# Layer 0's attention: q's product and the turned values change places in a ring of three PSUM banks, and the ring's empty place moves ahead of v's second chunk

## The chip, the cores and the metric

The kernel runs on one core of a Trainium2 chip as one program. The metric is the device time of one execution in microseconds (us). Three runs of the kernel before took 2770.33, 2770.84 and 2774.33 us; the median is 2770.84 us.

## The reference, cut to what matters

The model has four layers, each a cross attention and a feed-forward net on x of 16 batches x 112 rows x 256. Only the attention of layer 0 is touched. For each batch b it computes, with 8 heads of 32:

```
xn = layernorm(x)                       # 112 x 256
q  = xn @ wq.T + bq ; k = ctx @ wk.T + bk ; v = ctx @ wv.T + bv   # ctx: 375 x 256
p  = softmax(q k^T / sqrt(256)) ; o = p v                         # per head
res = o + q ; ln = layernorm(res) * g + b
out = silu(ln) @ base_w.T + b_splines(ln) @ (spline_w * scaler).T # 8 spline bases per value
x  = x + tanh(gate) * out
```

The values and the sums are the same before and after the change.

## The kernel before, in words

The program goes through eight stages one after the other (attention and net of each of four layers). In the attention of layer 0 (`attention_stage` with `kan=True`) each engine runs an instruction list of its own, written out batch by batch by `batches`; they meet only at semaphores. TensorE (PE) does all products and transposes, ScalarE (ACT) and VectorE (DVE) copy the results out of PSUM and do the softmax, the norms and the splines' arithmetic, GpSimd (POOL) does powers, squares and sums.

The stage is a software pipeline. In round t the program works on several batches at once: it turns (transposes) the probabilities of batch t and multiplies them with the values, prepares batch t+1 (`xT`, `k`, `q`, `v`, `qtok`), finishes the attention output of batch t-1 (`oback`, `lnt`) and does the splines of batch t-2 (`kan`). `LAG` says which batch a use belongs to. Rounds run from -1 to 17; in rounds 2 to 14 all uses are there.

A round has two halves, one for each group of four heads, and each half has the positions 0 to 3. The head of a half is `scores` (L807) and `pv` (L838). At positions 1 to 3 stands one `turn` each (four transposes of probabilities, L820), followed by the uses that the table `CYCLES` lists there:

- `xT`: the normed rows turned (L727). `k` (L712, four matrix products) and `v` (L720, four) of one chunk. `q` (L735, eight). `qtok`: q turned back to rows (L742, two).
- `oback`: the attention output turned back to rows (L758, two). `lnt`: the normed residual turned (L763, two). `kan`: the product with silu (L773, four), and right behind `lnt` the 32 spline products (L780).

All these results go through three PSUM banks, `full_ps`, in a strict ring: the n-th place of the list gets bank n mod 3. `rest` is a place that holds nothing and only moves the count on. `bank_free` makes PE wait before each use until the previous content of that bank is copied out. Who copies:

- ACT, in a fixed order in the first half: `xT` (L903), the first turn (L938), `o` out of its own bank (L946), the exponentials of heads 0 and 1 (L931), `k` (L892), the exponential of head 2, `q` (L921), that of head 3, `v` (L898), `k`. At a round's end, behind the splines' arithmetic, the two `v` of position 3.
- DVE, in the first half: two maxima of scores (L1152), one cube (L1245), the second turn's copy (L1172), `oback` (L1198), the third turn's copy (L1172), the sum with `qtok` and the statistics, a second cube, silu (L1240). In the second half: two maxima, the normed residual (L1214) that `lnt` needs, the turn's copy, and at the round's end the update of x (L1188, it reads `kan`), the last turn's copy (L1172), the next normed rows (L1075), `qtok` (L1103), statistics (L1193) and the rows of the net's norm (L195).

The lists of ACT and DVE put `oback` and `q`, and `qtok` and `v`, on different engines, so they don't depend on the order of these in `CYCLES`.

Of the kernel before, what the change touches and what calls it, by code (L numbers as in the profile page):

```python
# [222 lines left out]
def batches(eng, body, tail):  # L223

    for b in range(-1, B + tail):
# [3 lines left out]


CYCLES = {
    0: [[[("xT",)], [("k", 0)], [("q", 0), ("oback",)], [("v", 0, 0), ("k", 1)]],
        [[], [], [("kan",), ("lnt",)], [("v", 1, 0), ("qtok",), ("v", 2, 0), ("rest",)]]],
# [2356 lines left out]
```

How the kernel before makes its waits and increments, by code:

```python
    def settle(self, dve, b, count):  # L173
        core = self.core
        dve.bn_aggr(core.mv[:, b, :], core.row_stats[:, b, :]).then_inc(self.s_mv.sem, 1)
        dve.wait_ge(self.s_mv.sem, count + 1)
        if self.layer == 2:
            dve.tensor_scalar(core.rstd[:, b], core.mv[:, b, 1:2], 1.0 + RMS_EPS, EPS * RMS_EPS, ALU.mult, ALU.add)\
                .then_inc(self.s_var.sem, 1)
        else:
            dve.tensor_scalar(core.rstd[:, b], core.mv[:, b, 1:2], EPS, None, ALU.add).then_inc(self.s_var.sem, 1)
# [1 line left out]
    def root(self, pool, b, count):  # L185
        pool.wait_ge(self.s_var.sem, count + 1)
        pool.tensor_tensor(self.core.rstd[:, b], self.core.rstd[:, b], self.core.minus_half[:], ALU.pow)\
            .then_inc(self.s_root.sem, 1)
# [1 line left out]
    def apply(self, eng, b, count):  # L191
        core = self.core
        eng.wait_ge(self.s_root.sem, count + 1)
        eng.tensor_scalar(core.normed[:, b, :], core.x_all[:, b, :], core.mv[:, b, 0:1], core.rstd[:, b, :],
                          ALU.subtract, ALU.mult).then_inc(self.s_rows.sem, 1)
# [11 lines left out]
    def rows_in(self, eng, b):  # L208
        if b >= EARLY:
            eng.wait_ge(self.s_rows.sem, b - EARLY + 1)
# [330 lines left out]
                def load(b, par, known):  # L542
                    if known:
                        sp.wait_ge(s_job.sem, s_job.at(b - 2, index_of[kv[-1]]))
                        sp.sem_inc(s_tick[2].sem, 1)
                        sp.dma_start(ctxT[:, par], dram["ctxT"][b]).then_inc(s_ctx[par].sem, 16)
```

## Time and profile before

| | |
|---|---|
| median of three runs | 2770.84 us |
| the profiled execution | 2773.1 us, its span 2771.3 us |
| attention of layer 0 | about 10 to 410 us of the span |
| one round in its steady part | 21.7 us |
| PE busy over the whole span | 95% |

The profile is of one execution. Times in rows count from the start of the span. "[0.19 <-ACT a_qT L921]" behind a row is the idle time of the engine right before it and what ended it. PE's ends are modelled, so on PE the distance from one start to the next tells more than the durations. "PEld" is PE's weight load, and L numbers are lines of the kernel.

### The profile page before, as it was taken

Reading aid. Unit: us, or ns where it says so; the run is one execution under the profiler, and the core shown is the slowest. Engines: PE = TensorE matmul, PEld = TensorE weight load, DVE = VectorE, ACT = ScalarE, POOL = GpSimd, SP = SyncE. Lnnn points to the kernel's source line nnn. Section 1 sums busy time; section 2 is a strip of 40 time slices with the busy share of each in tenths; the row PEclk is TensorE's granted clock in tenths of the full one; section 3 lists DMA queues with packets and bytes.
Section 4 is the critical chain, followed back from the end, with each engine's and each line's share of the span. In section 5 each row is a group of like instructions: output and inputs, shape, how many; then the busy total and the mean of one; then the engine's idle time right before and its main releaser. Section 6 shows DMA issues by size and latency. Waiting matters only on the chain. (4 is left out here: it accounts for less than half of the span.)

```text
span 2771.3 us, 56714 instructions
## 1 busy us (share of the span) xinstructions
PE 2625.3 (95%) x19818; PEld 1983.4 (72%) x19818; DVE 1544.7 (56%) x4177; ACT 1301.0 (47%) x3610; POOL 643.8 (23%) x626
## 2 busy tenths in 40 slices
PE   6999978999999999989899998999998999979998
PEld 4777755666666666656666666999996777768887
DVE  4778746555555555536777774333325777842222
ACT  4777733343334434421566663333335777732222
POOL 1666661000000000000444431222221111113332
PEclk9999989999999999989999998999999999999999
DMA  4000002000000000010000006999992000059896
GB/s 124 18 18 18 12 16 94 13 13 7 13 7 13 7 13 7 1 34 1 21 18 20 22 7 219 330 325 332 326 328 58 24 18 24 7 197 311 304 313 224
DMA packets 91811, 267.57 MB, mean 97 GB/s; under 512 B 25068, under 2 KB 50804, under 8 KB 77268
## 3 DMA queue, kind: packets, MB, share of 16 engines
q1 hardware_dynamic: 74356, 242.53, 25.3%
q0 software_dynamic: 13632, 18.62, 3.1%
q10 hardware_dynamic: 3616, 3.67, 0.4%
q8 instruction: 128, 2.10, 0.3%
q14 instruction: 79, 0.65, 0.1%
HBM read 248.13 MB, written 16.65 MB: 96 GB/s over the span
## 5 line engine op out<-in xcount | busy, mean ns | idle before, releaser
L820 PEld LDWEIGHTS a_full_ps<-ident,a_probs 112*125 112x125 f32 x2688 | 367.0, 189 | 129.7 <-issue 64.5
L1917 PEld LDWEIGHTS m_banks<-m_x_inT,m_w 128*128 128x128 f32 x3824 | 435.1, 192 | 15.2 <-issue 13.5
L1917 PE MATMUL m_banks<-m_x_inT,m_w 128*128 128x128 f32 x3824 | 442.2, 276 | 1.4 <-ACT m_x_inT L1988 0.9
L931 ACT ACTIVATE a_probs<-a_masked,a_negmax 112x375 f32<-112x375 f32 x512 | 305.4, 598 | 287.7 <-DVE a_negmax L1146 287.7
L820 PE MATMUL a_full_ps<-ident,a_probs 112*125 112x112 f32 x2688 | 417.3, 281 | 18.3 <-ACT a_pT L938 5.6
L1172 DVE COPY a_pT<-a_full_ps 125x448 f32<-125x448 f32 x448 | 277.5, 621 | 222.1 <-PE a_full_ps L820 217.2
L720 PE MATMUL a_full_ps<-attention_room 128*125 128x256 f32 (+1 forms) x960 | 331.1, 474 | 9.8 <-ACT a_qT L921 3.9
L712 PE MATMUL a_full_ps<-attention_room 128*128 128x375 f32 x896 | 324.0, 490 | 13.8 <-PEq L1760 8.6
L1146 DVE CUSTOM_DVE_ANT_0 a_masked<-a_sc_ps,a_mask_add 112x375 f32<-112x375 f32 x512 | 249.8, 545 | 33.2 <-PE a_sc_ps L807 32.0
L931 ACT ACTIVATE a_probs<-a_sc_ps,a_negmax 112x375 f32<-112x375 f32 x384 | 217.0, 577 | 91.1 <-DVE a_negmax L1152 91.1
L838 PEld LDWEIGHTS a_o_ps<-a_pT,a_v 125*32 125x32 f32 (+1 forms) x5376 | 164.5, 118 | 126.5 <-issue 98.1
L807 PE MATMUL a_sc_ps<-a_kT,a_qT 32*112 32x375 f32 (+1 forms) x1792 | 241.7, 514 | 7.2 <-ACT a_probs L931 3.8
L1928 PE MATMUL m_banks<-m_w,m_hid 128*128 128x256 f32 x992 | 232.9, 383 | 0.0
L720 PEld LDWEIGHTS a_full_ps<-attention_room 128*125 128x125 f32 x960 | 165.9, 189 | 89.8 <-issue 65.6
L838 PE MATMUL a_o_ps<-a_pT,a_v 125*32 125x112 f32 (+1 forms) x5376 | 216.3, 265 | 6.3 <-DVE a_pT L1172 2.6
L712 PEld LDWEIGHTS a_full_ps<-attention_room 128*128 128x128 f32 x896 | 159.8, 194 | 84.9 <-issue 15.5
L1152 DVE TENSOR_REDUCE a_negmax<-a_sc_ps 112x2 f32<-112x750 f32 x192 | 171.2, 933 | 79.1 <-PE a_sc_ps L807 79.1
L2002 ACT ACTIVATE m_silu<-m_banks,m_b 128x128 f32<-128x128 f32 x280 | 102.7, 368 | 239.4 <-PE m_banks L1917 231.7
L1928 PEld LDWEIGHTS m_banks<-m_w,m_hid 128*128 128x128 f32 x992 | 179.9, 190 | 32.0 <-issue 11.9
L2146 DVE SCALAR_TENSOR_TENSOR m_hid<-m_banks,m_b,m_silu 128x128 f32<-128x128 f32 x280 | 98.0, 351 | 157.8 <-ACT m_silu L2002 157.8
L2002 ACT ACTIVATE m_silu<-m_banks 128x128 f32<-128x128 f32 x216 | 59.6, 276 | 213.0 <-PE m_banks L1917 213.0
L938 ACT ACTIVATE a_pT<-a_full_ps 125x448 f32<-125x448 f32 x224 | 120.0, 536 | 62.6 <-PE a_full_ps L820 61.1
(253 smaller groups left out, 3451.8 us busy)
## 6 DMA issues: line engine op xcount, KB each, us to landing
m_w<-in_L2f_w SPq DMA_DIRECT2D x105, 1024.0 KB, 6.8
m_w<-in_L3f_w SPq DMA_DIRECT2D x72, 768.0 KB, 4.8
attention_room<-in_ctxT SPq DMA_DIRECT2D x64, 375.0 KB, 3.1
m_w<-in_L3f_w SPq DMA_DIRECT2D x36, 640.0 KB, 5.6
m_b<-in_L2f_b SPq DMA_DIRECT2D x35, 128.0 KB, 7.9
p_rows<-normed SPq DMA_DIRECT2D x16, 224.0 KB, 6.3
attention_room<-in_L0x_spline_wT SPq DMA_DIRECT2D x1, 2048.0 KB, 10.3
net_room<-in_L1f_w SPq DMA_DIRECT2D x2, 1024.0 KB
```

Of the source, the lines that this page charges most:

```text
L712: mm = pe.matmul(use_ps[:, 0:SK], wk[:, c, u[1] * P:(u[1] + 1) * P], ctxT[:, par, c, :], start=(c == 0), stop=(c == DC - 1))
L720: mm = pe.matmul(use_ps[0:KT, 0:v_width], ctxT[:, par, c, k * KT:(k + 1) * KT], wv[:, c, part * v_width:(part + 1) * v_width], start=(c == ...
L807: pe.matmul(sc_ps[:, a, 0:SK], lhs, kT[r:r + k, par, c, :], start=True, stop=True)\
L820: mm = pe.transpose(full_ps[0:KT, bank_of["turn", i, k], (j % 4) * S:(j % 4 + 1) * S], probs[:, i % 2, a, t * KT:(t + 1) * KT], ident[0:S, ...
L838: mm = pe.matmul(o_ps[a % WIDE * VW:(a % WIDE + 1) * VW, block * S:(block + 1) * S], v[:, par, t, head(i, a), :], pT[:, i % 2, KC * a + t, :],
L931: act.activation(probs[:, i % 2, a, 0:SK], src, ACT.Exp, bias=negmax[:, m:m + 1], scale=-1.0 if mask else 1.0, accum_out=rowsum[:, par, n: ...
L1146: dve.tensor_tensor_reduce(out=masked[:, i % 2, a, :], in0=sc_ps[:, a, 0:SK], in1=bias, scale=-1.0, scalar=FLT_MAX, op0=ALU.add, op1=ALU.m ...
L1152: dve.tensor_reduce(negmax[:, m:m + 2], sc_ps[:, 2 * a:2 * a + 2, 0:SK], AX.X, ALU.max, negate=True).then_inc(s_max.sem, 1)
L1172: dve.tensor_copy(pT[:, i % 2, 4 * k:4 * (k + 1), :], full_ps[0:KT, bank_of["turn", i, k], 0:4 * S] .rearrange("p (j s) -> p j s", j=4)).t ...
L1917: mm = pe.matmul(ab_ps[:, (par * FC + f) % RING, i * SLOTS:(i + 1) * SLOTS], w[:, par, c, f * P:(f + 1) * P], x_inT[:, c, :], start=(c == ...
L1928: mm = pe.matmul(y_ps[:, par, 0:D], hid[parts[f], f, :], w2[parts[f], par, f, :], start=(f == 0), stop=(f == FC - 1))
L2002: act.activation(silu[parts[f], i, :], ab_ps[0:r, i, 0:SLOTS], ACT.Silu, bias=b1[0:r, par, f:f + 1] if biased else 0.0).then_inc(s_silu.se ...
```

## The change

Two lists of layer 0's table change; no other line does.

```
CYCLES = {
-    0: [[[("xT",)], [("k", 0)], [("q", 0), ("oback",)], [("v", 0, 0), ("k", 1)]],
-        [[], [], [("kan",), ("lnt",)], [("v", 1, 0), ("qtok",), ("v", 2, 0), ("rest",)]]],
+    0: [[[("xT",)], [("k", 0)], [("oback",), ("q", 0)], [("v", 0, 0), ("k", 1)]],
+        [[], [], [("kan",), ("lnt",)], [("rest",), ("v", 1, 0), ("v", 2, 0), ("qtok",)]]],
```

`v 0` is v's first chunk, `v 1` its second. The order of PE's work follows the list: `oback` is now ahead of `q`, and `qtok` behind `v 2`. The banks follow as well (T is a turn):

```
before  xT0 T1 k0:2 T0 q:1 oback:2 T0 v0:1 k1:2 | T0 T1 kan:2 lnt:0 T1 v1:2 qtok:0 v2:1 rest:2
after   xT0 T1 k0:2 T0 oback:1 q:2 T0 v0:1 k1:2 | T0 T1 kan:2 lnt:0 T1 rest:2 v1:0 v2:1 qtok:2
```

So these waits on a bank change: `oback` waited for k0's copy and now for the first turn's; `q` waited for the first turn's copy and now for k0's; `v0` waited for q's copy and now for oback's; `k1` for oback's and now for q's; `v1` for kan's (the update of x) and now for lnt's; `qtok` for lnt's and now for kan's; the next round's `xT` for qtok's and now for v1's, and its `k0` for v1's and now for qtok's. No instruction is added or taken away.

## Rows read from the trace of the kernel before

**Rows 1.** Page, part 1: busy time of each engine over the span.
```profile
PE 2625.3 (95%) x19818; PEld 1983.4 (72%) x19818; DVE 1544.7 (56%) x4177; ACT 1301.0 (47%) x3610; POOL 643.8 (23%) x626
```

**Rows 2.** Windows: stretch, length, busy PE, PEld, DVE, ACT, POOL, granted clock, DMA share, GB/s.
```profile
200.00:340.00 140.00, 137.51 (x1057) 101.82 (x1060) 111.45 (x208) 103.23 (x233) 90.78 (x59) 1.00 0.06 18
39.00:42.00 3.00, 3.00 (x7) 2.06 (x7) 0.00 (x0) 0.64 (x3) 0.00 (x0) 0.50 0.03 5
```

**Rows 3.** Waits of PE, 0 to 400 us: total us, times, longest.
```profile
PE a_full_ps L720 <- ACT a_qT L921: 3.9, 16, 0.7
...
PE a_full_ps L720 <- DVE x_all L1188: 1.8, 12, 0.2
```

**Rows 4.** Timeline of PE, first half of a steady round: start, us, what.
```profile
247.21 0.59 PE L820 MATMUL a_full_ps<-ident,a_probs 112*125 112x112 f32 x4
247.63 1.06 PE L735 MATMUL a_full_ps<-a_xT,attention_room 128*128 128x112 f32 x8
...
248.55 0.43 PE L758 MATMUL a_full_ps<-ident,a_oT 128*112 128x128 f32 x2
248.82 0.59 PE L820 MATMUL a_full_ps<-ident,a_probs 112*125 112x112 f32 x4
...
249.60 1.13 PE L720 MATMUL a_full_ps<-attention_room 128*125 128x256 f32 x4 [0.19 <-ACT a_qT L921]
```

**Rows 5.** Timeline of ACT in the same half.
```profile
247.91 0.59 ACT L892 ACTIVATE a_kT<-a_full_ps,attention_room 128x375 f32<-128x375 f32 x1
...
248.91 0.63 ACT L921 ACTIVATE a_qT<-a_full_ps,attention_room 128x112 f32<-128x112 f32 x2
```

**Rows 6.** Timeline of DVE in the same round, up to the normed residual.
```profile
247.83 0.62 DVE L1172 COPY a_pT<-a_full_ps 125x448 f32<-125x448 f32 x1
...
249.45 0.62 DVE L1172 COPY a_pT<-a_full_ps 125x448 f32<-125x448 f32 x1
...
254.80 0.41 DVE L1214 TENSOR_SCALAR a_resn<-a_res,a_mv,a_rstd 112x256 f32<-112x256 f32 x1
```

**Rows 7.** Timeline: the residual turned in a late round, then in the steady one.
```profile
211.41 0.42 DVE L1214 TENSOR_SCALAR a_resn<-a_res,a_mv,a_rstd 112x256 f32<-112x256 f32 x1
...
211.97 0.38 PE L763 MATMUL a_full_ps<-ident,a_resn 112*128 112x112 f32 x2 [0.26 <-DVE a_resn L1214]
...
255.35 0.38 PE L763 MATMUL a_full_ps<-ident,a_resn 112*128 112x112 f32 x2
```

**Rows 8.** Timeline of PE at that round's end.
```profile
262.51 0.59 PE L820 MATMUL a_full_ps<-ident,a_probs 112*125 112x112 f32 x4
...
263.25 1.13 PE L720 MATMUL a_full_ps<-attention_room 128*125 128x256 f32 x4 [0.15 <-DVE x_all L1188]
...
264.22 0.38 PE L742 MATMUL a_full_ps<-ident,a_qT 128*112 128x128 f32 x2
264.44 1.03 PE L720 MATMUL a_full_ps<-attention_room 128*125 128x256 f32 x4
```

**Rows 9.** Timeline of DVE and POOL at that round's end.
```profile
263.14 0.62 DVE L1172 COPY a_pT<-a_full_ps 125x448 f32<-125x448 f32 x1
...
264.55 1.72 POOL L622 TENSOR_TENSOR a_sq<-a_near 128x896 f32<-128x896 f32 x1
264.66 0.41 DVE L1103 SCALAR_TENSOR_TENSOR a_qtok<-a_full_ps,attention_room 112x256 f32<-112x256 f32 x1
...
265.33 1.10 DVE L195 TENSOR_SCALAR normed<-x_all,mv,rstd 112x256 f32<-112x256 f32 x1
```

**Rows 10.** Timeline of PE and ACT in round 0.
```profile
34.55 1.50 PE L735 MATMUL a_full_ps<-a_xT,attention_room 128*128 128x112 f32 x8
...
37.09 0.57 ACT L892 ACTIVATE a_kT<-a_full_ps,attention_room 128x375 f32<-128x375 f32 x1
...
38.75 1.98 PE L720 MATMUL a_full_ps<-attention_room 128*125 128x256 f32 x4 [0.63 <-ACT a_qT L921]
```

**Rows 11.** Timeline of PE in round 2, the turned residual.
```profile
81.43 0.38 PE L763 MATMUL a_full_ps<-ident,a_resn 112*128 112x112 f32 x2 [0.84 <-DVE a_resn L1214]
```

## The prediction

> **What bounds the kernel now.** I read the page's busy times first. PE is busy for 95% of the span and no other engine comes near it [rows 1]. Next the windows of the changed stage: from 200 to 340 us PE is busy for 137.51 of 140 us at a granted clock of 1.00, the 2.4 GHz level [rows 2]. So in the steady rounds almost nothing can be won but PE's small waits, and every wait that is added on PE lengthens the round by itself. Third, PE's waits in the stage: the chunk products (L720) waited 16 times for q's copy and 12 times for the update of x, 3.9 and 1.8 us together [rows 3]. These are the waits of `v0` and `v1` that the change can take away. Last, the timeline of a steady round, since on PE the starts tell more than the flagged idle time.
>
> **The first half: q behind oback.** Take the true size of the old wait. Four turned blocks take 247.63 - 247.21 = 0.42 us from start to start when nothing stalls; the later four reach `v0` only 249.60 - 248.82 = 0.78 us after their start [rows 4]. The stall is thus 0.36 us, twice the flagged 0.19. It ends when q's copy ends (248.91 + 0.63 = 249.54 [rows 5]), 0.06 us before `v0`.
>
> After the change `oback` stands where q stood, at 247.63. It takes 248.82 - 248.55 = 0.27 us [rows 4], so q could start at 247.90. But q now has k0's bank, and ACT copies k0 from 247.91 to 248.50 [rows 5]. ACT does that copy behind two exponentials, and its order is not changed. With the same 0.06 us, q starts at 248.56. It takes 248.55 - 247.63 = 0.92 us, so the third turn starts at 249.48 and not at 248.82: 0.66 us late. The old order hid the same wait: oback also needed k0's copy, but q's 0.92 us stood in front of it.
>
> `v0` then follows at 249.48 + 0.42 = 249.90, 0.30 late. It no longer waits for q's copy. It waits for oback's copy on DVE, which comes right behind the copy that started at 247.83; even if all of this half of DVE is 0.3 late, that is done by about 249.2. `k1` waits for q's copy, which ends about 249.62 + 0.06 + 0.63 = 250.3 (q's last product ends 0.14 beyond its issue, by 1.06 against 0.92), and k1 is due 0.96 us behind v0, at 250.86. So on PE alone this half loses 0.30 us.
>
> DVE has a path of its own. Its copy of the third turn starts at 249.45, just behind the end of that turn on PE (248.82 + 0.59 = 249.41) [rows 4, 6], and from there it works without idle time through statistics, cube, silu and two maxima to the normed residual, 254.80 to 255.21 [rows 6]. `lnt` on PE starts at 255.35, 0.14 us behind it [rows 7]. Is that DVE's doing or PE's own pace? In the late round the residual ends at 211.83 and `lnt` starts 0.14 behind that too, there with a flagged wait [rows 7]. The same distance with and without a flag says that in the steady rounds DVE also sets it, with no slack to speak of. The third turn is 0.66 late, so this chain is, and `lnt` and all 32 spline products behind it. **The first half costs 0.66 us a round**, the bounds are 0.30 (if this chain has slack) and 0.66.
>
> **The round's end: v1 off kan's bank.** Turn to v1 is 263.25 - 262.51 = 0.74 us where 0.42 would do [rows 8], a stall of 0.32. `v1` now needs lnt's copy, done 7 us earlier, so the stall goes. What is late next is the last turn's copy on DVE (263.14 + 0.62 = 263.76 [rows 9]), and `v2` needs it at both orders. v1 would start at 262.93 and takes 264.22 - 263.25 = 0.97 [rows 8], so v2 comes at 263.90, against 263.82 for the copy: hidden, but by 0.08 us only. **This gives 0.32 us a round**, bounds 0.24 and 0.32.
>
> `qtok` behind v2 ends later: v2 at 263.90 plus v1's 0.97 plus 0.38 for the two transposes is 265.25, so DVE's copy of it goes from 264.66 to about 265.3 [rows 8, 9]. What is queued behind it is statistics (L1193), the net's rows (L195) and the next round's maxima. L195 ran from 265.33 to 266.43, while POOL's operation ended at 264.55 + 1.72 = 266.27 [rows 9]. I read that as DVE waiting for POOL, and then it ends at 266.43 anyway: the lateness of 0.64 vanishes. The Trainium skill has the reason in SBUF — State Buffer, the section with the drawing of the ports: VectorE and GpSimd lock one shared port pair for a whole instruction, and the loser blocks. By that rule the sum stays as it is, and without it the maxima would be 0.64 late. Even then the copy of the second turn, 247.83 to 248.45 [rows 6], moves by 0.64 plus the 0.32 by which PE is now ahead, and ends at 249.41, and the third turn, which needs that bank, still starts at 249.48. Either way the price is nothing, but a second limit stands close behind k0's copy.
>
> The SP queue's prefetch of ctx waits for the last v of a batch, which now comes 0.5 us earlier; it has rounds of time. The next `xT` and `k0` wait for copies that end over a microsecond before them. Price nothing.
>
> **The rounds.** A full steady round: +0.66 - 0.32 = +0.34 us. There are 12 (rounds 3 to 14): +4.1.
> Round 2: `lnt` waits 0.84 us for a DVE chain that hangs on the spline arithmetic, not on the third turn [rows 11], so it swallows q's loss, and the end gives 0.32: -0.3.
> Round 1: no splines, `lnt` hangs on the scores, so +0.3, and nothing is won at its end.
> Round 0: q ran from 34.55, at the low clock, and k0's copy, behind exponentials that came late, ends at 37.09 + 0.57 = 37.66 [rows 10]. q moves to 37.72, takes about 1.45 and is followed by the turn, some 0.8 at the low clock: v0 at about 39.9 where it started at 38.75. I take +1.1. If the clock is high there, q takes 0.92 and v0 comes at 39.1, and from 39 to 42 us the clock was at its low level, 0.50 [rows 2], which a shifted pattern of idle time could take away or lengthen: bounds -1.4 (v0 +0.3, and 1.7 us of the low stretch gained) and +2.7.
> Round -1: q waits for k0's copy too, but x's load and the DVE behind it set round 0's start: 0. From round 15 on no q, k or v is left, and the order of the rest is the same: 0, with up to 1 us either way by the clock in the pipeline's emptying.
>
> Sum: 4.1 - 0.3 + 0.3 + 1.1 = **+5.2 us**. The profiled execution took 2773.1 us (span 2771.3), so it would take 2778.3. It lies 2.3 us over the median of the runs; the median goes from 2770.84 to **2776.1 us**, or 0.19% more. A change under 0.2% (5.5 us) is what a measurement of this kernel hardly tells from nothing, so I stand at the edge.
>
> In TensorE: Matmul & The Clock Gate, section "HAM oscillation", the Trainium skill says that waits between bursts of products keep PE falling back to its low clock. The row of 39 to 42 us agrees for the filling of the pipeline; by that rule round 0 would tend to its upper bound, +2.7, and the sum to 6.8. In the steady rounds the clock was at 1.00 with waits of 0.36 us, and 0.66 is not of another kind.
>
> **Rivals.**
> - *The waits only go.* If ACT's copy of k0 came early enough, or q's wait were covered, both stalls vanish: 13 x 0.32 at the ends and 15 x 0.36 in the first halves, less 5 to 9 us in all, as `lnt` may keep part: about 2763. For it: both waits are real and seen in each round. Against: k0's copy ends 0.6 us after q could start, in every steady round, and nothing before it on ACT moves.
> - *Both sides cancel.* DVE's chain to `lnt` has slack, so a round costs 0.30 - 0.32, about nothing, and only round 0 counts: 2770 to 2773. For it: the steady rounds have no flagged wait at `lnt`. Against: the equal distance of 0.14.
> - *Slower, by the second limit.* v2 misses its 0.08 us or the copy of the second turn comes after 249.42, so that the third turn waits for DVE. From 0.1 us of lateness beyond these on, each round loses that on top; with 0.3 us for 12 rounds it is 3.6 more, 2780. For it: DVE is 0.64 later at the round's end. Against: POOL's lock hides it.
>
> **Numbers.** The forecast's mechanism (+3 to +7.5) 0.55, the second limit 0.12, cancelling 0.20, waits only gone 0.13. The forecast lies half on each side of 5.5 us; with the second limit and the upper half that makes slower 0.40, the lower half and cancelling make the same 0.47, faster 0.13. The range of 8 in 10 is 2765 to 2781: it holds the forecast, cancelling and most of the second limit, and leaves out the full gain.
>
> **What would show it.** In a steady round of the changed kernel: q's eight products (L735) with a wait for ACT's a_kT (L892) of some 0.6 us from oback's end; no wait of L720 for a_qT or x_all; the third turn 2.27 us behind the second and not 1.61; `lnt` still 0.14 us behind L1214; L195 ending where POOL's operation ends; a round of 22.04 us and not 21.7. The prediction is wrong if q shows no wait, if `lnt` loses its tie to L1214, or if round 0 moves by more than 3 us.

## The result: 0.23% slower, and the profile after

The changed kernel took 2778.92 us (median of nine runs, 2778.26 to 2781.49), the one before 2774.06 us in nine runs beside it (2770.33 to 2775.34). The two medians lie 4.9 us (0.18%) apart; the ratio, estimated from all the runs, is 1.0023 (95% interval 1.0015 to 1.0032). The interval is clear of 1, so the change made the kernel slower; it also holds 1.002, so whether it is more or less than the 0.2% at which the prediction drew its line is not shown. The profiled execution took 2779.04 us (span 2777.2), 5.9 us above the one before; the forecast was 5.2 us.

The page of the kernel after, part 1, answers to [rows 1]: TensorE's busy time fell by 3 us while the span grew by 6, so what was added is idle time of TensorE.
```profile
PE 2622.4 (94%) x19818; PEld 1980.1 (71%) x19818; DVE 1540.8 (55%) x4177; ACT 1302.6 (47%) x3610; POOL 643.4 (23%) x626
```

Windows after, the same columns as [rows 2]: busy PE went from 137.51 to 134.37 of 140 us, at the same clock.
```profile
200.00:340.00 140.00, 134.37 (x1023) 99.61 (x1022) 103.95 (x200) 103.70 (x225) 90.87 (x58) 1.00 0.06 18
```

Waits of PE after, 0 to 400 us (total us, times, longest). Both rows of [rows 3] are gone; the first of these stands in their place, and the second grew from 3.1 us in 5 waits.
```profile
PE a_full_ps L735 <- ACT a_kT L892: 11.5, 16, 3.4
PE a_full_ps L763 <- DVE a_resn L1214: 5.8, 16, 0.7
```

Timeline after, first half of a steady round (its `xT` starts at 250.29). It answers to [rows 4 to 7].
```profile
252.26 0.59 PE L820 MATMUL a_full_ps<-ident,a_probs 112*125 112x112 f32 x4
252.68 0.38 PE L758 MATMUL a_full_ps<-ident,a_oT 128*112 128x128 f32 x2
252.96 0.59 ACT L892 ACTIVATE a_kT<-a_full_ps,attention_room 128x375 f32<-128x375 f32 x1
...
253.60 1.15 PE L735 MATMUL a_full_ps<-a_xT,attention_room 128*128 128x112 f32 x8 [0.53 <-ACT a_kT L892]
254.58 0.60 PE L820 MATMUL a_full_ps<-ident,a_probs 112*125 112x112 f32 x4
255.02 1.04 PE L720 MATMUL a_full_ps<-attention_room 128*125 128x256 f32 x4
255.22 0.62 DVE L1172 COPY a_pT<-a_full_ps 125x448 f32<-125x448 f32 x1 [1.20 <-PE a_full_ps L820]
...
260.57 0.42 DVE L1214 TENSOR_SCALAR a_resn<-a_res,a_mv,a_rstd 112x256 f32<-112x256 f32 x1
...
261.13 0.38 PE L763 MATMUL a_full_ps<-ident,a_resn 112*128 112x112 f32 x2 [0.34 <-DVE a_resn L1214]
```
The chain can be followed downward. ACT's copy of k0 ends at 252.96 + 0.59 = 253.55; q starts 0.05 later, though `oback` (252.68 + 0.27) would have let it go at 252.95. The third turn is 254.58 - 252.26 = 2.32 us behind the second (before 1.61). DVE, idle for 1.20 us until then, takes it up, and the residual and `lnt` come later by the same amount, 0.14 us apart as before. `v0` (L720) has lost its wait but starts 0.38 later.

Distances from the start of `xT`, read from such timelines of both kernels:

| start of | before | after | shift |
|---|---|---|---|
| third turn | 3.57 | 4.29 | +0.72 |
| `v0` (L720) | 4.35 | 4.73 | +0.38 |
| normed residual (L1214) | 9.55 | 10.27 | +0.72 |
| `lnt` (L763) | 10.12 | 10.84 | +0.72 |
| `v1` (L720) | 18.01 | 18.42 | +0.41 |
| next `xT`, the round | 21.70 | 22.12 | +0.42 |

From `lnt` to `v1` 0.31 us are won back, the stall of [rows 8]. The same positions stand, within 0.02 us, in every round from 3 to 14 but round 8, which is 0.35 us longer in all the kernels ([rows 7] show its residual at 211.41).

Timeline after, end of a round, DVE and POOL; it answers to [rows 9].
```profile
248.21 1.74 POOL L622 TENSOR_TENSOR a_sq<-a_near 128x896 f32<-128x896 f32 x1
...
248.86 0.42 DVE L1103 SCALAR_TENSOR_TENSOR a_qtok<-a_full_ps,attention_room 112x256 f32<-112x256 f32 x1 [0.45 <-PE a_full_ps L742]
...
249.53 0.56 DVE L195 TENSOR_SCALAR normed<-x_all,mv,rstd 112x256 f32<-112x256 f32 x1
```
L195 took 1.10 us before and takes 0.56 now, and again ends (250.09) 0.14 us behind the end of POOL's squares (249.95). It started later and was held for less, so against POOL, and through POOL against `lnt`, what follows it did not move. In one round this cover was missing; that is told further down, under the stretches of the stage.

### The profile page after: what moved, and what is told of

Read it like the earlier page. It is cut to its first block and busy times, and to the rows that moved or that the text cites. A ratio compares the mean times of both kernels' runs of the same rounds, so it can differ in the third digit from the quotient of the medians.

```text
span 2777.2 us, 56715 instructions
## 1 busy us (share of the span) xinstructions
PE 2622.4 (94%) x19818; PEld 1980.1 (71%) x19818; DVE 1540.8 (55%) x4177; ACT 1302.6 (47%) x3610; POOL 643.4 (23%) x626
## 5 line engine op out<-in xcount | busy, mean ns | idle before, releaser
L720 PE MATMUL a_full_ps<-attention_room 128*125 128x256 f32 (+1 forms) x960 | 327.6, 473 | 3.8 <-DVE a_pT L1172 2.5
L720 PEld LDWEIGHTS a_full_ps<-attention_room 128*125 128x125 f32 x960 | 166.2, 189 | 82.5 <-issue 66.2
```

The source lines that it names most:

```text
L720: mm = pe.matmul(use_ps[0:KT, 0:v_width], ctxT[:, par, c, k * KT:(k + 1) * KT], wv[:, c, part * v_width:(part + 1) * v_width], start=(c == ...
```

## Experiments

A "steady round" below is the distance that the starts of `xT` keep in rounds 4 to 13 of the profiled execution, round 8 left out. Times are medians of the runs of one sitting, ratios are against the kernel before in the same sitting.

### Each half of the change alone

e1_swap_only has the first half only:
```
-    0: [[[("xT",)], [("k", 0)], [("q", 0), ("oback",)], [("v", 0, 0), ("k", 1)]],
+    0: [[[("xT",)], [("k", 0)], [("oback",), ("q", 0)], [("v", 0, 0), ("k", 1)]],
```


> Only the first half of the change: oback ahead of q, the round's end as before. A steady round was 21.70 us before and 22.12 after the whole change. Theory (q's wait for k0's copy costs 0.72 us a round, the end gives 0.31 back): the round is 22.43 us, the third turn 2.3 us behind the second, and the time 8 to 11 us over the kernel before. Rival (the loss comes from the round's end, where qtok's copy is later and DVE with it): q's wait is cover for nothing and the round is about 21.7 to 21.8, the time within 2 us of the kernel before.

Measured: a round of 22.41 us, 2779.8 us, ratio 1.0026 (1.0016 to 1.0037). The swap alone costs 0.71 us a round.

e2_end_only has the second half only:
```
-        [[], [], [("kan",), ("lnt",)], [("v", 1, 0), ("qtok",), ("v", 2, 0), ("rest",)]]],
+        [[], [], [("kan",), ("lnt",)], [("rest",), ("v", 1, 0), ("v", 2, 0), ("qtok",)]]],
```


> Only the second half of the change: the empty place ahead of v1, qtok behind v2, q ahead of oback as before. Theory: v1's stall of 0.31 us goes and nothing else moves, so the steady round is 21.39 us and the time about 4 us (13 x 0.31) under the kernel before; the wait for q's copy (0.19 flagged) stays. Rival (qtok's lateness of 0.64 us reaches the maxima and delays the turn's copies): the round is 21.7 or more, up to 22.1, and the time not under that of the kernel before.

Measured: a round of 21.65 us where 21.39 was expected, 2772.75 us, ratio 1.0002 (0.9993 to 1.0011). This expectation failed. The stall of `v1` does go, but the round gets only 0.05 shorter. Added to the swap the same edit is worth 22.41 - 22.12 = 0.29. The two halves don't add up, so something else holds the round at 21.65. Round 3, the first full one, did take 21.40 as expected, with L1206 at 0.41 us; from round 4 on it is 21.65.

Timeline of e2_end_only, DVE, POOL and PE in one round:
```profile
269.06 2.08 POOL L636 TENSOR_TENSOR a_bases<-a_near 128x896 f32<-128x896 f32 x1 [1.15 <-DVE a_near L1245]
...
270.78 0.65 DVE L1206 TENSOR_TENSOR a_res<-a_res,a_qtok 112x256 f32<-112x256 f32 x1
...
276.38 0.38 PE L763 MATMUL a_full_ps<-ident,a_resn 112*128 112x112 f32 x2 [0.18 <-DVE a_resn L1214]
```
DVE's sum with `qtok` (L1206) takes 0.65 us and not the 0.41 it takes in the kernel before. It starts at 270.78, while POOL's sum runs to 271.14, and ends 0.29 us behind that. `lnt` is at 10.37 us from `xT` instead of 10.12. The same two operations in the kernel before:
```profile
247.99 2.08 POOL L636 TENSOR_TENSOR a_bases<-a_near 128x896 f32<-128x896 f32 x1 [1.15 <-DVE a_near L1245]
...
249.99 0.41 DVE L1206 TENSOR_TENSOR a_res<-a_res,a_qtok 112x256 f32<-112x256 f32 x1
```
There POOL's sum ends at 250.07 and DVE's at 250.40, 0.33 us behind (0.30 to 0.33 in the steady rounds). In e2, e3, e4, e8 and e9, where L1206 is longer than 0.42, it ends 0.27 to 0.30 behind POOL's sum. So the kernel before had only a few hundredths of a microsecond to spare at this place, and e2 and e3 gain 0.05 and 0.04 a round. In e2 L1206 ends 0.26 us later from `xT` than in the kernel before, and 21.39 + 0.26 is the 21.65 measured.

The POOL side of that round shows where POOL is kept: the row of L188, the power of the net's norm, stands right between the power of the next norm (L572) and the squares.
```profile
280.40 0.15 DVE L1068 TENSOR_SCALAR a_rstd<-a_mv 112x1 f32<-112x1 f32 x1
...
280.63 0.55 POOL L572 TENSOR_TENSOR a_rstd<-a_rstd,minus_half 112x1 f32<-112x1 f32 x1 [4.54 <-DVE a_rstd L1068]
281.14 0.55 POOL L188 TENSOR_TENSOR rstd<-rstd,minus_half 112x1 f32<-112x1 f32 x1
281.66 1.68 POOL L622 TENSOR_TENSOR a_sq<-a_near 128x896 f32<-128x896 f32 x1
```
This also shows how the loop closes. DVE's L1068, which releases POOL, stands in DVE's list behind the splines' distances, which need `lnt`'s copy: from `lnt` to POOL's L572 it is 4.25 us here and 4.24 in the kernel after.

e3_end_qtok_kept keeps `qtok` where it was and moves only the empty place, `[("rest",), ("v", 1, 0), ("qtok",), ("v", 2, 0)]`, with q ahead of `oback`.

> The empty place ahead of v1, but qtok stays between v1 and v2 (v1 in bank 0, qtok 1, v2 2); q ahead of oback as before. Theory (qtok's place costs nothing, since the net's rows on DVE wait for POOL anyway): 21.39 us a round as with qtok moved, about 4 us under the kernel before. Rival (qtok's lateness costs something): this kernel's round is shorter than that with qtok moved, by 0.1 us or more.

Measured: a round of 21.66 us, 2770.07 us, ratio 0.9991 (0.9982 to 1.0). This expectation failed as well, and in the same way (round 3 took 21.34): `qtok`'s place is not what eats the gain. Over the whole kernel e3 is 2.7 us faster than e2, though their steady rounds are equal; one wait at the stage's end, told further down, is 1.7 us longer in e2.

### q's wait taken away by ACT's order

e4_k0_copied_first is the whole change, and ACT copies k0 ahead of the exponentials of heads 0 and 1:
```
+                    copies(t, par, 0, 1)
                     for group in groups:
                         exps(*group, (0, 1))
-                    copies(t, par, 0, 1)
```


> The whole change, and ACT copies k0 ahead of the two exponentials instead of behind them. Theory (k0's copy behind the exponentials is the whole cause): q starts about 0.5 us earlier (k0's products end 2.12 us behind xT's start, plus 0.06, 0.58 and 0.06: q at 2.8 and not at 3.31), the steady round is 21.6 us, round 0 loses its 2 us, and the time is 1 to 2.5 us under the kernel before. Rival (the second turn's copy on DVE is a second limit at the same spot, or the later exponentials cost the same elsewhere): the round stays at 22.0 to 22.1 and only round 0 gains.

Measured: a round of 21.66 us, 2771.16 us, ratio 0.9995 (0.9986 to 1.0004). Timeline of e4_k0_copied_first, PE and ACT in one round:
```profile
268.85 0.57 ACT L892 ACTIVATE a_kT<-a_full_ps,attention_room 128x375 f32<-128x375 f32 x1 [0.49 <-PE a_full_ps L712]
...
269.08 0.38 PE L758 MATMUL a_full_ps<-ident,a_oT 128*112 128x128 f32 x2
...
269.48 1.15 PE L735 MATMUL a_full_ps<-a_xT,attention_room 128*128 128x112 f32 x8
```
The copy ends at 269.42 and q starts at 269.48, 0.40 behind `oback` instead of 0.92. So it is ACT's copy of k0 that the change waits for, and its lateness is that of the exponentials ahead of it. The loss in the rounds goes with it, and the round stops at the same 21.65 as in e2 and e3, though q and v0 are in other places.

### The second loop

e5_end_and_pool_order is e3, and POOL does the net's norm ahead of the power of the next norm:
```
+                    if early(t - 3):
+                        net_rows(t - 3)
                     if exists(t + 2):
                         power(t + 2)
-                    if early(t - 3):
-                        net_rows(t - 3)
```


> The empty place ahead of v1 with qtok kept between v1 and v2, and on POOL the power for the net's rows goes ahead of the power for the next batch, into an idle stretch of 4.5 us, so that the squares and cubes start 0.5 us earlier. Theory (the floor of 21.65 us is a loop over POOL: squares and cubes, DVE's cube, POOL's sum of bases, which holds up DVE's sum with qtok, the residual and lnt): the floor sinks by up to 0.5 us and the round is what the third turn's chain allows, 21.36 to 21.42; the time 4 to 6 us under the kernel before. Rival (the residual is late for another reason in DVE's own list): the round stays at 21.65 and the time at that of the kernel without the edit on POOL.

e6_pool_order_only is the kernel before with that edit alone.

> The kernel before with nothing but the other order of the two powers on POOL. Theory (in the kernel before the third turn's chain and v1's stall set the round, POOL's loop has 0.05 us of slack): 21.70 us a round, within 1 us of the kernel before. Rival (POOL's work sets the round already): 21.2 to 21.6.

e7_half_bases is e3, and POOL adds the bases of the first chunk for four of the eight splines only; the products of that chunk read these four twice, so part of the net's result is changed. It shortens one operation of POOL and leaves the order alone.
```
-                    pool.tensor_tensor(bases[:, c], near2[:, c], near1[:, c], ALU.add).then_inc(s_kp.sem, 1)
+                    n = 4 if c == 0 else 8
+                    pool.tensor_tensor(bases[:, c, 0:n], near2[:, c, 0:n], near1[:, c, 0:n], ALU.add).then_inc(s_kp.sem, 1)
```


> The empty place ahead of v1 with qtok kept, POOL's order as before; POOL's sum for the first chunk adds only four of the eight bases (the products read these four twice), so it takes about 1.05 us and not 2.08. Part of the computation is changed: bases 5 to 8 of the first chunk are replaced by 1 to 4. Theory (this sum, running when DVE wants to add qtok, is what makes the residual late): DVE's sum with qtok is back at 0.41 us and the round at 21.36 to 21.42. Rival: 21.65.

Measured: e5 has a round of 21.34 us and took 2765.52 us, ratio 0.9979 (0.9970 to 0.9988). e6 has 21.69 us and took 2772.58 us, ratio 1.0001 (0.9992 to 1.001). e7 has 21.42 us; its one run took 2766.82 us beside the 2772.34 of the kernel before.

Timeline of e5_end_and_pool_order:
```profile
264.87 2.09 POOL L636 TENSOR_TENSOR a_bases<-a_near 128x896 f32<-128x896 f32 x1 [1.15 <-DVE a_near L1245]
...
267.02 0.42 DVE L1206 TENSOR_TENSOR a_res<-a_res,a_qtok 112x256 f32<-112x256 f32 x1
...
272.05 0.59 POOL L188 TENSOR_TENSOR rstd<-rstd,minus_half 112x1 f32<-112x1 f32 x1
```
Timeline of e7_half_bases (its lines have one number more, L637 and L1207 are L636 and L1206 of the others):
```profile
267.83 1.14 POOL L637 TENSOR_TENSOR a_bases<-a_near 128x448 f32<-128x448 f32 x1 [1.15 <-DVE a_near L1246]
...
269.55 0.42 DVE L1207 TENSOR_TENSOR a_res<-a_res,a_qtok 112x256 f32<-112x256 f32 x1
```
Two unlike edits, one that takes L188 from ahead of the squares and one that makes the sum itself 0.94 us shorter, both bring L1206 back to 0.42 us and shorten the round by 0.32 and 0.24. The same order of POOL without the end's edit (e6) gains nothing. So there are two loops of almost one length: PE with the stall of `v1`, 21.70, and POOL's squares and cubes, DVE's cube, POOL's sum, the sum with `qtok`, the residual and `lnt`, 21.65. Removing one alone leaves the round at the other.

### The order with both, and the change with POOL's order

e8_turn_before_q is e5 with k0 copied first by ACT, as in e4, and another order of places, `oback`, third turn, q, `v0`:
```
-    0: [[[("xT",)], [("k", 0)], [("q", 0), ("oback",)], [("v", 0, 0), ("k", 1)]],
+    0: [[[("xT",)], [("k", 0)], [("oback",)], [("q", 0), ("v", 0, 0), ("k", 1)]],
```


> On top of the empty place ahead of v1 and POOL's order: ACT copies k0 ahead of the exponentials, and on PE the order is oback, third turn, q, v0 (banks 1, 2, 0, 1). Theory: the third turn needs k0's copy, done 2.77 us behind xT's start, so it comes at 2.83 and not at 3.57; q needs the second turn's copy and starts at 3.3, v0 has no stall. DVE's chain to the residual is then 0.3 to 0.4 us earlier, and PE's own work sets the round at about 21.2 us; round 0 is 0.5 us shorter too; the time 5 to 8 us under the kernel before. Rival (POOL's sum or the copy of the second turn holds the chain): 21.4 or more, no gain over the kernel with the end and POOL's order alone.

Measured: a round of 21.15 us, 2766.41 us (2759.3 to 2769.26), ratio 0.9981 (0.9972 to 0.999). The round is 0.19 us shorter than e5's, read from the fastest of its eleven runs; the times of the two cannot be told apart. Both are faster than the kernel before and the kernel after. e5 reaches it by two small edits, without the swap.

Timeline of e8_turn_before_q: the sum with `qtok` meets POOL's sum again.
```profile
264.11 2.08 POOL L636 TENSOR_TENSOR a_bases<-a_near 128x896 f32<-128x896 f32 x1 [1.15 <-DVE a_near L1245]
...
265.64 0.83 DVE L1206 TENSOR_TENSOR a_res<-a_res,a_qtok 112x256 f32<-112x256 f32 x1
```

e9_change_pool_order is the whole change with e5's order of POOL.

> The whole change and POOL's order of the two powers. Theory (with oback ahead of q the round is set by q's wait for k0's copy and by the third turn's chain, and POOL's loop of 21.65 us lies 0.47 us under it): the round stays at 22.12 us, with 0.53 us of wait ahead of q. Rival (POOL's loop has a part in the change's loss): 21.6 to 22.0.

Measured: a round of 23.04 us where 22.12 was expected; its one run took 2789.74 us beside 2771.88. The expectation failed, by 0.92 us a round. Timeline of e9_change_pool_order:
```profile
251.11 1.74 POOL L622 TENSOR_TENSOR a_sq<-a_near 128x896 f32<-128x896 f32 x1
...
252.97 2.30 DVE L195 TENSOR_SCALAR normed<-x_all,mv,rstd 112x256 f32<-112x256 f32 x1
253.03 2.09 POOL L627 TENSOR_TENSOR a_near<-a_sq,a_near 128x896 f32<-128x896 f32 x1 [0.18 <-POOL a_sq L622]
...
257.89 1.15 PE L735 MATMUL a_full_ps<-a_xT,attention_room 128*128 128x112 f32 x8 [1.39 <-ACT a_kT L892]
```
POOL's squares end at 252.85, and its cube starts at 253.03. DVE's L195 is shown from 252.97 on, inside that gap, and ends at 255.27, 0.15 us behind the cube. The maxima that stand behind it are late, ACT's exponentials with them, the copy of k0 behind these, and q waits for 1.39 us.

e10_same_qtok_kept is e9 with `qtok` in its old place ahead of the last v.

> The run before (whole change and POOL's order: a round of 23.04 us) with one difference: qtok goes back between v1 and v2. Theory (there qtok's copy came so late that DVE asked for the net's rows at 252.97, 0.12 us behind the end of POOL's square, and stood 2.30 us behind POOL's next product): with qtok early the rows are done in 0.4 to 1.1 us, the maxima are on time, q's wait is back at 0.53 us and the round at 22.1 us. Rival (the swap of oback and q together with POOL's order is at fault, whatever qtok does): the round stays at 23 us.

Measured: a round of 22.07 us; its one run took 2775.18 us beside 2774.05. Timeline of e10_same_qtok_kept:
```profile
244.68 1.73 POOL L622 TENSOR_TENSOR a_sq<-a_near 128x896 f32<-128x896 f32 x1
...
245.63 0.93 DVE L195 TENSOR_SCALAR normed<-x_all,mv,rstd 112x256 f32<-112x256 f32 x1
246.59 2.08 POOL L627 TENSOR_TENSOR a_near<-a_sq,a_near 128x896 f32<-128x896 f32 x1 [0.18 <-POOL a_sq L622]
...
250.56 1.15 PE L735 MATMUL a_full_ps<-a_xT,attention_room 128*128 128x112 f32 x8 [0.53 <-ACT a_kT L892]
```
With `qtok` early L195 comes 0.78 us before the squares end (246.41), is held until then and passes ahead of the cube. The 0.92 us are back, and the rival that blames the swap together with POOL's order falls.

## Why the prediction was right, step by step

The direction, the size and the main mechanism came out. The prediction itself gave slower only 0.40 and the same 0.47, with its line at 5.5 us, and the result stands on that line too: the medians differ by 4.9 us, the ratio makes 6.4 of 2774. (Its median after, 2776.1, is 2776.0 by its own sum, 2770.84 + 5.2.) One step, the price of a late `qtok`, and one line of the sum, the emptying, were wrong, and part of the closeness is luck.

**q waits for k0's copy: right.** Forecast 0.66 us a round for the third turn and `lnt`, measured 0.72. The missing 0.06 is q's own length: it is 0.98 from start to start behind a wait and 0.92 in the old place. e1 shows the cost alone (0.71) and e4 shows the cause: with the copy earlier the loss is gone.

**DVE's chain to `lnt` has no slack: right.** The 0.14 us between residual and `lnt` stayed, now with a flagged wait of 0.34. The rival in which both sides cancel needed slack there and falls; so does the one in which the waits only go.

**v1's stall goes: right in the change, and not a property of the edit.** 0.31 us measured, 0.32 forecast. But e2 and e3 show that it pays only because q's wait has made the round longer than the second loop: 21.65 against 22.12. In the old first half the same edit gives 0.05. My working had no step for that loop. It read DVE's chain to `lnt` as fed by the third turn alone and left out the other thing that L1206 meets, POOL's sum, which ended 0.08 us after the start of L1206 in the kernel before.

**`qtok` late, covered by POOL: right in the steady rounds, wrong in the last one.** In rounds 3 to 13 L195 ended behind POOL's operation as forecast. What I priced for the case of no cover, "nothing", was wrong in kind. In the steady rounds of the change L195 came 0.42 us before the end of the squares. In e9 it came 0.12 us after, and then it was not late by 0.64 but by a whole operation of POOL, 2.30 us where L1214, of the same form, takes 0.42, and the round lost 0.92. The rival of the second limit had this direction with 0.3 us a round for a price; in the steady rounds it did not occur, and it would have been three times as dear. In round 14 it did occur, once, for 1.7 us (below). The Trainium skill, SBUF — State Buffer, section "SBUF: two separate sides", calls the shared port pair an exclusive lock which the first to start holds for the whole instruction. The rows of e9 and e10 agree that the wait is for a whole instruction, 2.30 against 0.93 us. On who comes first the row of e9 does not show it: L195 is shown 0.06 us ahead of the cube (spans on POOL are rough), and it was L195 that waited.

**The rounds.** Shift of the kernel after against before, by stretch of the profiled executions:

| stretch | forecast | measured |
|---|---|---|
| rounds -1 and 0 | +1.1 | +0.2 +2.1 |
| rounds 1 and 2 | 0.0 | -0.2 |
| rounds 3 to 14 | 12 x 0.34 = +4.1 | 12 x 0.42 = +5.1 |
| emptying of the pipeline | 0 | +1.5 |
| the rest of the program | 0 | -2.8 |
| sum | +5.2 | +5.9 |

The row of rounds 1 and 2 hides two shifts of `xT`, +1.8 and -2.0. The prediction priced the next `xT`'s wait at nothing. At the start of round 2 it is not nothing: `xT` waits 0.90 us there for ACT's copy of `v1`. But in the kernel before the turn right behind `xT` waited 1.20 us for ACT's copy of `v2`, so the wait has only changed its place. By the starts of that turn (70.57 and 73.19) the two rounds moved by +0.3 and -0.5, near the +0.3 and -0.3 forecast.

Round 0 was under-sized by 1 us, within its bounds. Windows of before, then of after, in the columns of [rows 2]:
```profile
38.00:44.00 6.00, 5.37 (x35) 3.13 (x37) 0.91 (x2) 2.21 (x8) 0.00 (x0) 0.72 0.01 3
```
```profile
38.00:44.00 6.00, 5.85 (x19) 4.89 (x20) 0.62 (x1) 2.19 (x8) 0.00 (x0) 0.50 0.01 3
```
Timeline of after, PE in round 0; it answers to [rows 10].
```profile
38.15 2.05 PE L735 MATMUL a_full_ps<-a_xT,attention_room 128*128 128x112 f32 x8 [3.38 <-ACT a_kT L892]
...
40.83 1.94 PE L720 MATMUL a_full_ps<-attention_room 128*125 128x256 f32 x4
```
From 36 to 38 us, in q's wait, the granted clock was still 0.97. After the 3.38 us of waiting it stands at its low level, 0.50, for all of the six microseconds in which before it averaged 0.72. `v0` comes 2.1 us late where I had said 1.1. About 0.4 of the missing 1.0 is q itself, 1.84 us from start to start and not 1.45, at the low clock; another 0.4 is q's start, at 38.15 and not 37.72, half of it because the round itself began 0.2 late. The first part is the direction of the clock rule that I had weighed and left out of the sum.

The emptying's +1.5 comes from `qtok`'s new place. Timelines of round 14's end and the turn that follows, before and then after:
```profile
352.08 0.40 DVE L195 TENSOR_SCALAR normed<-x_all,mv,rstd 112x256 f32<-112x256 f32 x1
...
352.33 2.08 POOL L627 TENSOR_TENSOR a_near<-a_sq,a_near 128x896 f32<-128x896 f32 x1 [0.18 <-POOL a_sq L622]
...
356.58 0.66 PE L820 MATMUL a_full_ps<-ident,a_probs 112*125 112x112 f32 x4 [0.82 <-DVE a_pT L1172]
```
```profile
359.82 2.09 POOL L627 TENSOR_TENSOR a_near<-a_sq,a_near 128x896 f32<-128x896 f32 x1 [0.18 <-POOL a_sq L622]
...
360.12 1.94 DVE L195 TENSOR_SCALAR normed<-x_all,mv,rstd 112x256 f32<-112x256 f32 x1
...
365.43 1.04 PE L820 MATMUL a_full_ps<-ident,a_probs 112*125 112x112 f32 x4 [2.49 <-DVE a_pT L1172]
```
In round 14 there is no batch two ahead any more, so POOL has one power less to do, and its cube starts earlier in the round. L195 now comes 0.30 us behind the cube's start, is held to 0.15 us behind its end, and the maxima, the cube on DVE and the turn's copy follow late. PE's wait for that copy grows by 1.67 us: the shift against the kernel before is 7.18 us at the product ahead of it and 8.85 at this turn. Behind it stretches at the low clock, not the same ones in both kernels, move it up and down, and it ends at 8.7. The runs separate it: the wait is 2.48 to 2.49 us in all four kernels with `qtok` behind `v2` (after, e2, e4, e9) and 0.81 to 0.82 in seven with `qtok` in its old place (before, e1, e3, e5, e6, e7, e10). (e8 has another order of banks, and its turn has no such wait.) So the step of the prediction that priced `qtok`'s lateness at nothing was wrong by 1.7 us, at a place where it had allowed up to 1 us for the clock alone.

The last row was not foreseen either, and takes back most of what the stage lost beyond the forecast. The first product of the stage behind (L1475) came 8.7 us late, and the span ended 5.9 late. The rows that show the 2.8 us given back are the sources of two lines, before and then after: L753 runs from layer 1's attention on, L2285 behind it. The columns after the count are shortest, mean and longest in ns, and the times of the first and the last.
```profile
L753 PE MATMUL a_full_ps<-attention_room,a_oT x384: 377/379/740, 545.5 to 2431.3; 128*112 128x256 f32 x192
L2285 PE MATMUL d_y_ps<-net_room,d_hid x256: 377/379/470, 1221.5 to 1317.3; 128*112 128x256 f32 x128
```
```profile
L753 PE MATMUL a_full_ps<-attention_room,a_oT x384: 377/379/740, 554.2 to 2437.2; 128*112 128x256 f32 x192
L2285 PE MATMUL d_y_ps<-net_room,d_hid x256: 377/379/470, 1227.4 to 1323.3; 128*112 128x256 f32 x128
```
Between the two marks lie 676.0 us before and 673.2 after, of work that the change does not touch. The windows around the emptying of that attention, before and after, shifted by 8.7 us so that they hold the same work, show the clock:
```profile
1170.00:1190.00 20.00, 13.70 (x101) 11.24 (x98) 7.49 (x23) 4.42 (x12) 0.55 (x1) 0.64 0.00 1
```
```profile
1178.70:1198.70 20.00, 13.70 (x105) 11.22 (x102) 7.53 (x24) 4.42 (x12) 0.55 (x1) 0.74 0.00 1
```
Between these marks the kernel before, e2, e6 and e9 show 675.9 to 676.1 us, the one after, e1, e3, e4, e5 and e8 673.1 to 673.6, e7 and e10 673.9 to 674.1. Each is one execution, and executions of one kernel lie as far apart (2770.33 to 2775.34 us for the one before), so it is not shown that the 2.8 us belong to the change. The profiled total came out near the forecast partly by luck: the stage itself is 3.5 us worse than I said (1.2 in rounds -1 and 0, 1.0 in the steady rounds, 1.5 in the emptying, less 0.2), and 2.8 came back elsewhere. Why the clock falls at another place of the same work was not tried.

## What to carry to other kernels

Before a stall is priced as a gain, look for a second loop of nearly the same length: an operation on another engine that already runs a few hundredths of a microsecond beside the one you free. Two edits that are worth nothing alone (e3's and e6's, 0.04 and 0.01 us a round) gave 0.36 us a round together. An order in which a copy stands behind other work on its engine decides which bank may be used next, so in a ring price a swap by the ends of the copies. And where VectorE is covered by an operation of GpSimd, the price of losing the cover was what was left of GpSimd's next operation (2.30 us in e9, 1.94 in round 14 of the change), not the lateness. Look for that in the last rounds of a pipeline too, where an engine with less to do runs ahead.

## What the runs showed of the hardware that was not expected

A VectorE operation that comes in the gap of 0.18 us between two GpSimd operations may lose to the second: L195 was shown from 0.06 us ahead of the cube and still took 2.30 us (e9); shown 0.25 us ahead of it, in round 14 of the kernel before, it took 0.40. With 0.42 us (after) or 0.78 us (e10) to go in the first operation it was held to its end and went first. The sum with `qtok`, which reads two operands of SBUF, was held too (0.41 us free, 0.65 in e2, 0.83 in e8), each time beside POOL's sum of bases, and each time it ended 0.27 to 0.30 us behind that sum.
